# The head of the first cross attention: who stacks the first keys, when the output weights are masked, where the second octet's maxima stand, and where the late queries are split

## The reference, cut to what matters

```python
def _L0_xattn_ref(query, key, value, wq, bq, wk, bk, wv, bv, wo, bo):
    q = query @ wq + bq          # query = layernorm(x), 16 x 64 x 128
    k = key @ wk + bk            # key = value = ctx_1024, 16 x 1601 x 128
    v = value @ wv + bv          # 16 heads of 8 features
    att = softmax(q k^T / sqrt(8))
    return (att v) @ wo + bo
x = x + _L0_xattn_ref(_layernorm(x), ctx_1024, ctx_1024, ...)
```

## Time and profile before

| what | value |
|---|---|
| median of three runs | 1934.91 us |
| the profiled execution | 1935.08 us |
| its span, first to last instruction | 1933.3 us |
| granted TensorE clock over the span | 0.945 of full |
| TensorE busy | 1710.4 us, 88% of the span |
| VectorE busy | 1233.6 us, 64% |
| ScalarE busy | 857.0 us, 44% |
| GpSimd busy | 526.8 us, 27% |

### The profile page before, as it was taken

One profiled execution on the slowest core, in us unless ns is written; L12 is line 12 of the kernel. 1 busy time (PEld: TensorE's weight loads), 2 busy tenths in 40 slices (PEclk: granted clock), 3 DMA queues, 4 the chain that ended last, 5 costly groups with the idle time before them and its releaser, 6 DMA issues. The chain is left out here.

```text
span 1933.3 us, 33380 instructions
## 1 busy us (share of the span) xinstructions
PE 1710.4 (88%) x11692; PEld 1210.4 (63%) x11692; DVE 1233.6 (64%) x3059; ACT 857.0 (44%) x1939; POOL 526.8 (27%) x708
## 2 busy tenths in 40 slices
PE   6998999999988993599999999999999999999423
PEld 3665666666667883466766666666666676665322
DVE  7666666666655774666666656666666666653577
ACT  2555555555552441344444444444444444442222
POOL 2000000000012222324553245423543345411223
PEclk8999999999998997799999999999999999999665
DMA  5533535353400112100000000000000000000000
GB/s 145 133 86 88 134 97 120 86 120 86 103 2 1 45 66 107 46 23 23 29 29 12 17 28 28 11 28 17 28 28 11 18 28 28 1 1 1 1 5 5
DMA packets 32659, 90.35 MB, mean 47 GB/s; under 512 B 8552, under 2 KB 17424, under 8 KB 32528
## 3 DMA queue, kind: packets, MB, share of 16 engines
q1 hardware_dynamic: 32384, 88.09, 16.9%
q10 hardware_dynamic: 144, 0.61, 0.2%
HBM read 40.43 MB, written 8.91 MB: 26 GB/s over the span
## 5 line engine op out<-in xcount | busy, mean ns | idle before, releaser
L2221 PE MATMUL c_pv_ps<-c_prob_t,c_xn 128*128 128x512 f32 (+2 forms) x896 | 413.4, 598 | 0.0
L340 ACT ACTIVATE c_prob<-c_score_ps,c_neg_max 128x512 f32<-128x512 f32 (+1 forms) x512 | 304.8, 608 | 64.3 <-PE c_scratch L2207 35.0
L986 DVE TENSOR_REDUCE a_chunk_max<-a_side_ps 128x1 f32<-128x512 f32 (+1 forms) x416 | 261.0, 665 | 112.2 <-PE a_side_ps L737 111.9
L359 DVE TENSOR_REDUCE c_chunk_max<-c_score_ps 128x1 f32<-128x512 f32 (+1 forms) x512 | 291.2, 581 | 48.6 <-PE c_score_ps L266 47.1
L237 PE MATMUL c_turn_ps<-consts,c_prob 128*128 128x128 f32 (+2 forms) x1792 | 286.4, 277 | 11.9 <-DVE c_prob_t L369 11.2
L237 PEld LDWEIGHTS c_turn_ps<-consts,c_prob 128*128 128x128 f32 (+2 forms) x1792 | 212.6, 140 | 97.2 <-issue 32.4
L2221 PEld LDWEIGHTS c_pv_ps<-c_prob_t,c_xn 128*128 128x128 f32 (+2 forms) x896 | 158.4, 191 | 164.6 <-issue 164.5
L373 DVE COPY c_prob_t<-c_turn_ps 65x128 f32<-65x128 f32 (+1 forms) x256 | 61.4, 279 | 298.6 <-PE c_turn_ps L237 298.6
L894 ACT ACTIVATE a_prob<-a_st_ps 128x1024 f32<-128x1024 f32 (+1 forms) x224 | 214.5, 958 | 53.9 <-PE a_st_ps L721 53.9
L266 PE MATMUL c_score_ps<-c_x_hi,c_q_hi 128*128 128x512 f32 (+1 forms) x512 | 218.6, 427 | 2.7 <-ACT c_prob L340 1.9
L324 ACT ACTIVATE c_prob_t<-c_turn_ps 128x512 f32<-128x512 f32 x128 | 76.4, 597 | 276.1 <-PE c_turn_ps L237 274.4
(11 more groups left out here) (318 smaller groups left out, 2595.5 us busy)
## 6 DMA issues: line engine op xcount, KB each, us to landing
a_stack<-a_k_hi SPq DMA_DIRECT2D x126, 200.1 KB, 4.1
a_stack<-a_k_lo SPq DMA_DIRECT2D x63, 200.1 KB, 4.2
a_ctx<-in_ctx_dram SPq DMA_DIRECT2D x16, 768.0 KB
c_ctx<-in_ctx_dram SPq DMA_DIRECT2D x16, 768.0 KB
absorbed_queries<-b_q_out SPq DMA_DIRECT2D x16, 512.0 KB, 3.4
c_q_raw<-absorbed_queries SPq DMA_DIRECT2D x16, 512.0 KB, 3.3
w<-in_L_ffn_w_dram SPq DMA_DIRECT2D x2, 512.0 KB
fold_raw<-in_L_xattn_Wkv_dram SPq DMA_DIRECT2D x2, 512.0 KB
```

The costliest lines, as they stand in the source:

```text
L340: nc.scalar.activation(prob[s % 2][:, cols], score_ps[:, cols], ACT.Exp, bias=neg_max[:, s % 2:s % 2 + 1], accum_out=sums[:, (s // QUAD) % ...
L359: nc.vector.reduce_max(chunk_max[:, s % 2, c:c + 1], score_ps[:, quad_chunk(c, keys)], AX_X).then_inc(chunk_max_done, 1)
L986: nc.vector.reduce_max(out, rows, AX_X).then_inc(side_taken, 1)
L2221: last = nc.tensor.matmul(lay.own.pv_ps[:], t.xn[m][0:rows, i, :], lay.own.prob_t[u][0:rows, i, :], start=(i == 0), stop=(i == LAT))
```

## The change

- Stacking for batch element 0. ScalarE issues no DMA any more. SyncE issues all twelve: first the four of high keys of groups 0 and 1, once all four chunks of `k_hi` are made, then the two of low keys, once `k_lo` is made, then the six of groups 2 and 3.
- The copy of the turned tokens goes from behind the fourth query split to behind the second.
- The two masking instructions go from ahead of the first maximum to behind the shift of octet 0.
- The six units of octet 1 in the head are gone from it; steps 0, 1 and 2 of octet 0 have four units instead of two.
- The late queries are split in octets 2, 4, 6 and 8, the high part at step 4, the low part at step 5, instead of octets 1, 3, 5 and 7 at step 5. TensorE's and ScalarE's part of these jobs stays where it was.

```diff
 def max_units_at(n, s):
+    if n == 0 and s <= 3:
+        return [("max", 1, i) for i in range(4 * s, min(4 * s + 4, UNITS))]
     octet, at = divmod(STEPS * n + s + 3, STEPS)
...
 def first_sides():
-    return [("max", 0, i) for i in range(UNITS)] + [("shift", 0)] + [("max", 1, i) for i in range(6)]
+    return [("max", 0, i) for i in range(UNITS)] + [("shift", 0)]
...
+            def stack_first_keys():
+                sp.wait_ge(k_high, CHUNKS)
+                sp.wait_ge(pads_set, 1)
+                for group in range(2):
+                    stack_part(0, group, 0)
+                    stack_part(0, group, 2)
+                wait_keys_done(sp, 0)
+                for group in range(2):
+                    stack_part(0, group, 1)
+                stack_keys(0, 1)
...
-            act.wait_ge(first_low[0], CHUNKS)
-            for i, part in enumerate((k_hi, k_lo, k_hi)):
-                nc.scalar.dma_start(stack[32 * i:32 * i + 32, 0, 1, 0:CTX].bitcast(F32), part[32:64, :].bitcast(F32)).then_inc(stacked[0], 16)
...
             for i in range(GROUPS):
                 dve.wait_ge(q_done, i + 1)
                 split_queries(i)
-            take_turned(1)
+                if i == 1:
+                    take_turned(1)
...
-            for i in range(2):
-                nc.vector.tensor_scalar(g.wo_half[:, :, i, :], wo_rows[:], ...).then_inc(wo_masked, 1)
             for side in sides[0:10]:
                 take_side(side)
...
             take_side(sides[UNITS])
+            for i in range(2):
+                nc.vector.tensor_scalar(g.wo_half[:, :, i, :], wo_rows[:], ...).then_inc(wo_masked, 1)
             dve.wait_ge(bias_made, 1)
...
-                    take_queries(job_at(n, s))
+                    if n in (2, 4, 6, 8) and s == 4:
+                        dve.wait_ge(job_taken, number["q", n // 2 - 1, 0] + 1)
+                        high_queries(GROUPS + n // 2 - 1)
+                    if n in (2, 4, 6, 8) and s == 5:
+                        low_queries(GROUPS + n // 2 - 1)
```

More of the change, by code:

```diff
@@ L619, in load_ctx, with stack_part @@
                              dram.ctx[b:b + 1, FULL * P:CTX, :].rearrange("o p d -> p (o d)")).then_inc(ctx_loaded, 16)
+            def stack_part(b, group, i):
+                part = (k_hi, k_lo, k_hi)[i]
+                sp.dma_start(stack[32 * i:32 * i + 32, b % 2, group, 0:CTX].bitcast(F32), part[32 * group:32 * group + 32, :].bitcast(F32)).then_inc(stacked[group // 2], 16)
             def stack_keys(b, u):
                 for group in (2 * u, 2 * u + 1):
-                    if b == 0 and group == 1:
-                        continue
-                    for i, part in enumerate((k_hi, k_lo, k_hi)):
-                        sp.dma_start(stack[32 * i:32 * i + 32, b % 2, group, 0:CTX].bitcast(F32), part[32 * group:32 * group + 32, :].bitcast(F32)).then_inc(stacked[u], 16)
+                    for i in range(3):
+                        stack_part(b, group, i)
+            def stack_first_keys():
[8 more added lines that the diff above has]
+                stack_keys(0, 1)
             sp.dma_start(g.x_tok[:], dram.x.rearrange("(t b) s d -> (b s) t d", b=2)).then_inc(loaded, 16)
@@ L650, in _ @@
                     load_ctx(b + 1)
+                if b == 0:
+                    stack_first_keys()
+                    continue
                 wait_keys_done(sp, b)
                 for u in range(QUADS):
-                    if b == 0 and u == 0:
-                        sp.wait_ge(pads_set, 1)
                     if b >= 2:
@@ L1010, in take_keys, with high_queries, low_queries @@
                                                ALU.add, ALU.subtract).then_inc(job_taken, 1)
[L1012 to L1016, removed]
+            def high_queries(i):
+                v, cols = i % GROUPS, slice(i // GROUPS * BANK, i // GROUPS * BANK + BANK)
+                nc.vector.tensor_copy(q_st[:, v, cols].bitcast(F32R), q_raw[i % 2][:]).then_inc(q_high, 1)
+            def low_queries(i):
+                v, cols = i % GROUPS, slice(i // GROUPS * BANK, i // GROUPS * BANK + BANK)
+                dve.wait_ge(q_high, i + 1)
+                nc.vector.tensor_tensor(q_st[64:ONES_AT, v, cols], q_raw[i % 2][64:ONES_AT], q_st[64:ONES_AT, v, cols],
+                                        ALU.subtract).then_inc(q_split, 1)
             def take_low_keys(b, c, bank):
@@ L1032, in split_queries @@
             def split_queries(i):
[L1033 to L1037, removed]
+                high_queries(i)
+                low_queries(i)
             sides = first_sides()
@@ L1080, in _ @@
             take_side(sides[UNITS])
+            for i in range(2):
+                nc.vector.tensor_scalar(g.wo_half[:, :, i, :], wo_rows[:], g.consts[:, C_HALFROWS + i:C_HALFROWS + i + 1], None,
+                                        ALU.mult).then_inc(wo_masked, 1)
             dve.wait_ge(bias_made, 1)
```

2 lines of the change are left out of this document (removed).

## The result

| | us |
|---|---|
| before, median of 6 runs (1932.0 to 1937.35) | 1934.71 |
| changed, median of 6 runs (1921.22 to 1927.9) | 1923.37 |
| ratio, 95% interval | 0.9944, 0.9929 to 0.9959 |
| changed, the same kernel run again, 6 runs (1917.8 to 1922.31) | 1919.73 |
| ratio of that, 95% interval | 0.9923, 0.9907 to 0.9939 |

The change makes the kernel faster by 0.6 to 0.8%. The forecast was 1920.7 us, between 1915 and 1928.

The account below looks back on a forecast made before the run. The prediction took TensorE as the bound where it has no gaps, and the head as a chain of waits. From 1935.08 us, -4.8 in the head and -9.6 from late splits gave 1920.7 us, range 1915 to 1928.

Parts of the forecast that it names:

- Late splits: Octets 2, 4, 6, 8: first two steps lose their 10.4 us excess, less 0.8 of stalls; net -9.6 us.
- the 0.8 us of stalls: Late splits in even octets: low part beside GpSimd's product stalls TensorE 0.2 us a time, +0.8 us in all.
- Rival 4: Late splits: low part and GpSimd's product exclude each other fully, four times 1.04 us; 1924.1 us; chance 0.10.
- Rival 3: Late splits return only plain waits, 6.5 us; low clock in octets 4 and 8 has another cause; 1923.8 us; chance 0.10.
- rival 5: A split in an even octet stalls TensorE over 1 us and brings the low clock; 1930.3 us; chance 0.05.
- First maximum: Head: stacking, copy and masking moves bring the first maximum to 24.8 us, 5.5 us earlier.
- The six maxima: Octet 0: six units leave the head (-3.75 us) and return in steps 0 to 2; net +0.7 us.
- the masking's stall of 0.5 us: Step 0 of octet 0: VectorE masks while TensorE would go on, charged at +0.5 us.
- The head: Stretch up to octet 1: first maximum -5.5 and six maxima +0.7 give -4.8 us, between -2.5 and -8.
- The sum: Whole kernel: 1935.08 less 4.8 in the head and 9.6 from late splits, 1920.7 us; later parts untouched.
- Rival 1: Clock stays at 1.00 through octet 0, so the head gains more; 1917.3 us; chance 0.15.
- Rival 6: Four-unit steps paced by VectorE drop the clock to 0.50 lastingly, about 1.5 us a step; slower, up to 1952; chance 0.03.

Follow-up runs that it names:

- units not parted: Parting, against the changed kernel: octet 0's four units a step split, two behind scores, one behind weighing, one behind the values job; 1917.84 us, again 1919.24.
- both halves at step 5: Changed kernel with high and low parts of each late query split both at step 5 of octets 2, 4, 6, 8; 1919.95 us.

## Why the prediction was right

The time and the main steps held. That it came within 0.2 us at octet 10 is in part luck: the errors of the terms offset each other.

- **Late splits, forecast -9.6.** The mechanism is shown by its run alone: 10.4 us, all of the excess in the earlier trace rows, the clock's part included. The step that was mis-sized is the 0.8 us of stalls beside GpSimd's product; they are zero. Rival 4, the exclusion in full with VectorE as the one that waits, is out. The low part started first in all four octets (93.36 in octet 2 of the changed kernel), and the one that was lengthened was GpSimd's product, from 1.04 to 1.25 us, for which TensorE has no wait there:

```profile
93.36 0.68 DVE L1033 TENSOR_TENSOR a_q_st<-fold_raw,a_q_st 32x512 f32<-32x512 f32 x1
```

```profile
93.69 1.25 POOL L694 TENSOR_TENSOR a_q_bd<-a_q_st,a_block_of 96x512 fp32r<-96x512 f32 x1 [5.88 <-PE a_st_ps L738]
```

  That whoever starts first keeps its time and blocks the other agrees with the page "SBUF — State Buffer" of the Trainium skill (section "SBUF: two separate sides"): 0.36 us of the low part were left when GpSimd's product started, and it took 0.22 us longer. What the prediction left out is the question who starts first, and whether the blocked one is awaited. Rival 3 is out as well, since no lower clock came in octets 1 to 10 once the gap was gone. So is rival 5: in the twelve executions with the late splits moved, no even octet from 2 to 8 was above 15.98 us.
- **First maximum, forecast 24.8, -5.5.** Measured 24.80. Half a microsecond of it is the execution's own: the first query projection stands at 16.32 before and at 15.80 after, 16.62 in the repeated run. Counted from there the first maximum moved from 14.00 to 9.00 and 9.10 us, so -5.0. The reasons held, and the new bound is the stack, as the row of 24.29 says. But the parts were weighed wrongly. The prediction gave the masking 2.17 and the issues 3.6, with the stack landing 0.3 us after VectorE is free. It lands 1.1 us after that here, and 0.7 to 2.0 us in the other executions with this head. So undoing one of the two moves alone loses less than its own time: 0.9 us with the masking back, 2.2 with the issues back (both rough, see the experiments). The new place of the copy has no run of its own. With the issues back and the copy in its new place TensorE's unit is ready before VectorE comes, so there it is not what bounds.
- **The six maxima, forecast +0.7.** Measured +0.7 by the run with the maxima back, +1.0 against before, and by the other executions 0.5 to 1.5 with the longer stretch of low clock. That it came out at 0.7 is partly luck, for the terms shifted: the waits for VectorE in the steps with four units are there (0.36 and twice 0.56 us), the masking's stall of 0.5 us is not, since it runs in 0.62 us beside an idle GpSimd. And the clock fell to 0.50 at the gap of the shift, as said, but from 38.8 for 6.8 us instead of 10.3, so step 2 and most of step 1 ran at the high one.
- **The head, forecast -4.8.** -4.25 at octet 1: -5.5 at the first maximum, +0.3 from there to the shift's end (14.22 us before, 14.50 now), +1.0 behind it. With the execution's own start taken out it is -3.7. Counted from the first projection, octet 1 starts after 49.7 and 50.4 us in the two executions with the old head, and after 46.6 to 47.1 in four with the new one and units not parted; in a fifth (both halves at step 5), with half as much of the lower clock, after 44.5. So the head's gain is 2.6 to 3.7 us with the usual clock, under the forecast.
- **The sum.** -14.4 forecast, -14.6 at octet 10, -12.3 in the span, -11.3 and -14.5 in the two sets of runs. The missing 2 to 3 us of the first set did not come again in the second, and the later stages vary by several microseconds between executions, in kernels that leave them as they are. The prediction's "later parts only start earlier" was right on average and said nothing of this width.
- **Rival 1**, the clock at 1.00 all through octet 0, came in none of the 14 profiled executions: the shortest stretch at the lower level there was 3.4 us, in three of them. The 0.5 us that it takes off the head beside the 5.5 and 2.2 come from no row. **Rival 6** did not come anywhere: in the changed kernel the clock rose at 45.6, in the midst of the steps with four units, and did not fall again before octet 10.

It is open what sets the clock's changes in the later stages of a given execution; no run tries it.

## What to carry to other kernels

A short instruction that waits for a young result stalls everything queued behind it on its engine, and the engine that waits for those pays in gap and, in part of the places, in clock. Move it to where its input is old, provided that its input stands in a buffer of its own. The queries had one (`q_raw`), the keys had not (the scratch bank), and the same move won 10.4 us with the one and lost with the other. An early input is worth only what the next bound leaves: two moves that freed VectorE 6.1 us earlier won 5.0, and undone one at a time they cost about 0.8 and 2.2. Four short products in a row against two banks are paced by the engine that empties them. Put other work of the first engine between them instead of moving them out of the head in a lump.

## What the runs showed of the hardware

- A gap of 1.2 us in TensorE's row was followed by a stretch of 3.4 us at the lower clock in two of four places in each of the two executions that had it, in octets 4 and 8 in one and in octets 2 and 6 in the other. It cost 1.5 us each. In the other twelve profiled executions, without the gap, no such stretch came in octets 1 to 10, although their odd octets have gaps of 0.65 us.
- Two 128x256 VectorE instructions took 2.17 us beside GpSimd's products and 0.62 us without.
- Where a split on VectorE and GpSimd's product overlap, the one that started first keeps its time, and the other takes longer by what was left of the first less about 0.14 us. GpSimd's product, behind the low part: 0.36 us were left and it took 0.22 more (changed kernel), 0.54 left and 0.40 more (both halves at step 5). VectorE's high part, behind the product: 0.60 left and 0.46 more (before, at 82.87).
- The twelve stacking parts of 200.1 KB landed 0.97 us apart on average when two engines issued them (before) and 0.90 us apart when SyncE alone did (changed). The sixth came 9.6 us after the last high keys were done in the three executions with two engines, and 8.3 to 9.5 us after them in the eleven with SyncE alone, which starts earlier.
